# Cross-attention on one core: eighteen blocks of up to 128 query rows in place of twenty heads of 112, with q and k stacked through DRAM

## The reference

```python
q    = heads(x @ W_q)                      # 20 heads, 112 x 16
k_t, v_t = heads(text @ W_k), heads(text @ W_v)        # text: 371 rows
probs_t  = softmax(q @ k_t.T * 0.25)                   # 112 x 371 per head
text_out = probs_t @ v_t
k_ip, v_ip = heads(ip @ W_k_ip), heads(ip @ W_v_ip)    # ip: 4 rows
qsem = l2norm(probs_t @ text)                          # 112 x 512 per head
fused = q @ k_ip.T * 0.25 + 0.5 * qsem @ l2norm(ip).T  # 112 x 4 per head
ip_out = (softmax(fused) * mask) @ v_ip
out = (text_out + ip_out) @ W_out + b_out + x
```

## Time and profile before

| | us |
|---|---|
| median of 3 runs | 786.95 |
| the profiled execution | 787.76 |
| its span, first to last instruction | 786.0 |
| PE busy in the span | 752.7 (96%) |
| PE weight loads | 589.2 (75%) |
| DVE busy | 661.3 (84%) |
| ACT busy | 583.6 (74%) |
| POOL busy | 445.5 (57%) |
| mean granted TensorE clock | 0.984 of 2.4 GHz |
| DMA engines | queue of SyncE 44.66 MB, 21.9% of 16 engines |

### The profile page before, as it was taken

How to read it: one execution, slowest core, us unless ns; L and a number is a source line. 1 busy time by engine, 2 the same in 40 slices (tenths; PEclk the granted TensorE clock), 3 DMA queues, 4 the chain that set the end, 5 groups by cost and what they waited for, 6 DMA issues and landing times.

```text
span 786.0 us, 23801 instructions
## 1 busy us (share of the span) xinstructions
PE 752.7 (96%) x7730; PEld 589.2 (75%) x7730; DVE 661.3 (84%) x1960; ACT 583.6 (74%) x1702; POOL 445.5 (57%) x558
## 2 busy tenths in 40 slices
PE   5899999999999999999999999999999999999983
PEld 3568778787877878787787878778787777878661
DVE  4878898988989898898989889898998989889883
ACT  4378787877878787787878778787877878777770
POOL 4035574656647465664746566474656647464762
PEclk8999999999999999999999999999999999999996
DMA  8313222221412223140222314022231402021000
GB/s 268 100 50 74 73 68 61 61 79 43 104 27 67 63 58 81 42 107 24 68 65 57 83 41 107 21 70 65 54 87 38 109 22 69 19 52 42 9 2 15
DMA packets 71465, 50.02 MB, mean 64 GB/s; under 512 B 16640, under 2 KB 71280, under 8 KB 71344
## 3 DMA queue, kind: packets, MB, share of 16 engines
q1 hardware_dynamic: 67648, 44.66, 21.9%
q10 hardware_dynamic: 3696, 3.84, 1.7%
HBM read 20.80 MB, written 2.38 MB: 29 GB/s over the span
## 4 chain that ended last, share of the span: by engine, by line
PE 91%; issue 2%; DVE 2%; POOL 2%; DMA 1%; ACT 1%; ACTq 0%; SPq 0%; POOLq 0%; DVEq 0%
PE ps_prep L475 22%; PE ps_gram L574 19%; PE ps_pT L556 13%; PE ps_gram L575 12%; PE ps_score L548 6%; PE ps_prep L530 5%; PE ps_val L582 2%; PE ps_val L584 2%; PE ps_prep L527 1%; PE ps_prep L505 1%; PE ps_prep L610 1%; PE ps_prep L507 1%; DMA xt_sb<-in_x_t 1%; POOL dual L407 1%; POOL nrm L417 1%
## 5 line engine op out<-in xcount | busy, mean ns | idle before, releaser
L407 POOL TENSOR_TENSOR dual<-prob 112x371 f32<-112x371 f32 x320 | 282.9, 884 | 302.4 <-ACT prob L753 283.2
L574 PE MATMUL ps_gram<-gram_hi,pT_hi 125*128 125x371 f16 (+1 forms) x960 | 303.9, 320 | 0.0
L575 PE MATMUL ps_gram<-gram_lo,pT_hi 125*128 125x371 f16 (+2 forms) x960 | 255.9, 267 | 0.0
L747 ACT ACTIVATE pT_hi<-ps_pT 125x336 f16<-125x336 f32 x320 | 144.6, 452 | 143.4 <-PE ps_pT L556 139.9
L737 ACT ACTIVATE prob<-ps_score,low 112x371 f32<-112x371 f32 x320 | 184.0, 575 | 16.3 <-DVE low L912 9.8
L912 DVE TENSOR_REDUCE low<-ps_score 112x1 f32<-112x371 f32 x320 | 171.3, 535 | 28.5 <-PE ps_score L548 24.8
L917 DVE TENSOR_TENSOR pT_lo<-ps_pT,pT_hi 125x336 f16<-125x336 f32 x320 | 160.0, 500 | 38.2 <-ACT pT_hi L747 34.0
L927 DVE CUSTOM_DVE_ANT_0 quad_junk<-ps_gram,dual 112x371 f32<-112x371 f32 x320 | 171.1, 535 | 12.4 <-PE ps_gram L575 6.0
L753 ACT ACTIVATE prob<-prob 112x371 f16<-112x371 f32 x320 | 168.9, 528 | 0.0
L582 PE MATMUL ps_val<-val,pT_hi 125*128 125x42 f16 (+1 forms) x960 | 166.8, 182 | 0.0
L556 PE MATMUL ps_pT<-ident,prob 112*125 112x112 f32 x960 | 156.9, 272 | 5.6 <-DVE pT_lo L917 3.7
(11 more groups left out here) (183 smaller groups left out, 1405.8 us busy)
## 6 DMA issues: line engine op xcount, KB each, us to landing
ctx_sb<-in_ctx_t SPq DMA_DIRECT2D x15, 750.0 KB, 4.5
k_st<-k_lo SPq DMA_DIRECT2D x62, 70.3 KB, 2.1
k_st<-k_hi SPq DMA_DIRECT2D x60, 70.3 KB, 2.1
q_st<-q_hi SPq DMA_DIRECT2D x64, 48.0 KB, 2.0
k_st<-k_lo SPq DMA_DIRECT2D x62, 46.9 KB, 2.0
q_st<-q_lo SPq DMA_DIRECT2D x60, 48.0 KB, 2.0
k_st<-k_hi SPq DMA_DIRECT2D x60, 46.9 KB, 2.0
x_sb<-in_x SPq DMA_DIRECT2D x16, 140.0 KB, 2.4
```

Source lines behind the costliest of these rows:

```text
L407: nc.gpsimd.tensor_tensor(dual[:, h % 2, :], prob[:, h % 4, 0:TX], prob_16[:, h % 2, :], ALU.subtract).then_inc(s_dual, 1)
L574: nc.tensor.matmul(ps_gram[h % 2][:, 0:TX], hi, gh[0:TROWS[i], i, :], start=(i == 0), stop=False, skip_group_check=True)
L575: last = nc.tensor.matmul(ps_gram[h % 2][:, i * TC:TX], hi, gl[0:TROWS[i], i, i * TC:TX], start=False, stop=(i == NT - 1), skip_group_chec ...
```

## The change

A batch becomes 18 blocks. Blocks 0 to 17 are heads 0 to 17. Heads 18 and 19 are each cut in seven strips of 16 query rows, and blocks 0 to 13 carry one strip in rows 112 to 127, beside the 112 rows of their own head. A block of two heads takes its value products for both heads (84 and 42 columns, a strided slice of val), and its copy out of ps_val too. After block 13 the strips' values, quadratic forms and image scores are moved to their places by 14 DMAs (move_rows). q and k go to DRAM in four DMAs and come back in 24, 16 partitions at a time, into stacks where a strip's q and k stand in the 16 partitions beside the own head's; the masks and the second copies of q_hi and q_lo go. Values are copied out in four groups of 6, 6, 2 and 4 blocks. The order of the pieces, the steps of make, take, split, finish and soft are set anew for 18 steps: the last piece is a gram, made whole in step 16. The norms and powers of heads 0 to 13 are taken in steps 14 to 17 of their own batch, those of the other six in the next. k_st1 lies over w_raw. The start no longer stacks with DVE copies.

```diff
+NB = 18
+XR = P - S            # 16 rows
+XP = S // XR          # 7 strips
+NBX = HX * XP         # 14 blocks of two heads
+GROUPS = ((0, 6), (6, 12), (12, NBX), (NBX, NB))
-PIECE_Q, PIECES_K, PIECES_V, PIECES_G = 0, (1, 2, 3), (5, 7, 9), (4, 6, 8)
+PIECE_Q, PIECES_K, PIECES_V, PIECES_G = 0, (1, 2, 3), (5, 7, 8), (4, 6, 9)
+WHOLE = (PIECE_Q, PIECES_K[-1], PIECE_TURN_G)
-SPLIT_STEP = {2: 0, 4: 1, 6: 2, 8: 3, 10: 4}
+SPLIT_STEP = {2: 0, 4: 1, 7: 2, 9: 3, 11: 4}
-FINISH_STEP = {12: 0, 14: 1, 16: 2, 18: 3}
+FINISH_STEP = {11: 0, 13: 1, 15: 2, 17: 3}
+EARLY_VALS_STEP, EARLY_NORM_STEPS, EARLY_POWS = 14, (15, 15, 15, 16), {16: (0, EARLY // 2), 17: (EARLY // 2, EARLY)}
+VALS_STEP, POW_STEP, EXP_STEP = 0, 2, 6
+Q_OUT_STEP, Q_IN_STEP, K_OUT_STEP, K_IN_STEP, MOVE_STEP, LOAD_X_STEP = 2, 4, 7, 9, 14, 13
...
+        def stack_k(eng, a, term):
+            src, dst, p0 = k_bounce[a.odd, term % 2], k_st[a.odd], 32 * term
+            eng.dma_start(dst[p0:p0 + DH, :, :], src[0:NB * DH].rearrange("(t p) s -> p t s", p=DH)).then_inc(s_kst[a.odd], 16)
+            for e in range(HX):
+                eng.dma_start(dst[p0 + DH:p0 + 2 * DH, e * XP:(e + 1) * XP, :],
+                              src[(NB + e) * DH:(NB + e + 1) * DH].unsqueeze(1).to_broadcast([DH, XP, T])).then_inc(s_kst[a.odd], 16)
...
+            def bounce_k(a):
+                if a.n >= 2:
+                    sp.wait_ge(s_kst[a.odd], STACKED * a.pair)
+                sp.wait_ge(s_prep_hi, NM * a.n + place(a, PIECES_K[-1]) + 1)
+                sp.wait_ge(s_kip, a.n + 1)
+                k_to_dram(sp, a, 0)
                 sp.wait_ge(s_prep_lo, NM * a.n + place(a, PIECES_K[-1]) + 1)
+                k_to_dram(sp, a, 1)
+            def bring_k(a, term):
+                reached(sp, s_score, NB * (a.n - 1))
+                sp.wait_ge(s_stack, 1 + a.odd)
+                sp.wait_ge(s_k_out[term % 2], 16 * (a.n + 1))
+                stack_k(sp, a, term)
+            def move_rows(b):
+                sp.wait_ge(s_half, len(GROUPS) * b.n + 3)
+                sp.wait_ge(s_quad, NB * b.n + NBX)
+                sp.wait_ge(s_ip_score, NB * b.n + NBX)
+                reached(sp, s_vals, b.n)
+                for j in range(XP):
+                    q0 = j * XR
+                    sp.dma_start(raw[q0:q0 + XR, NB:H, 0:2 * VW], raw[S:P, j:NBX:XP, 2 * VW:BW]).then_inc(s_moved, 16)
+                    sp.dma_start(meta[b.odd][q0:q0 + XR, NB:H, :], meta[b.odd][S:P, j:NBX:XP, :]).then_inc(s_moved, 16)
...
             def end(f, step):
                 if step == VALS_STEP:
+                    pool.wait_ge(s_half, len(GROUPS) * (f.n + 1))
+                    pool.wait_ge(s_moved, MOVED * (f.n + 1))
+                    sum_values(EARLY, H).then_inc(s_vals, 1)
...
-                    last = nc.tensor.transpose(ps_pT[0:TC, i * S:(i + 1) * S], prob[:, h % 4, i * TC:(i + 1) * TC],
-                                               ident[0:S, 0:S])
+                    last = nc.tensor.transpose(ps_pT[0:TC, i * r:(i + 1) * r], prob[0:r, g % 4, i * TC:(i + 1) * TC], ident[0:r, 0:r])
...
+                heads = slice(t, NB + t // XP + 1, NB + t // XP - t) if t < NBX else slice(t, t + 1)
...
+                    nc.tensor.matmul(out_, pT_hi[0:r, t % 2, i, :], v[0:r, i, heads, :], start=(i == 0), stop=False, skip_group_check=True)
...
+                for t in range(NB):
+                    if prepare and t == Q_OUT_STEP:
+                        bounce_q(b.next())
+                    if prepare and 0 <= t - Q_IN_STEP < 2:
+                        for term in range(2):
+                            bring_q(b.next(), 2 * (t - Q_IN_STEP) + term)
...
             split_weight(w_hi[:, :, 1, :], w_raw[:, :, 1, :], s_w[1], 1)
-            act.wait_ge(s_prep_hi, place(start, PIECES_K[-1]) + 1)
-            act.wait_ge(s_kip, 1)
-            for dst, src in k_restack(0, (0, 2)):
-                act.dma_start(dst, src).then_inc(s_kst[0], 16)
+            act.wait_ge(s_stack, 1)
+            act.wait_ge(s_k_out[1], 16)
+            for term in (1, 3):
+                stack_k(act, start, term)
             make_hi(start, PIECES_V[0], SETUP_BANKS)
```

More of the change, by code:

```diff
@@ L65, with rows, group, column @@
 SOFT_NORMS, SOFT_ARGS = 4, 10
-TEXT_OUT_STEP = 8
+EARLY_STEPS = 1 + SOFT_NORMS
+TEXT_OUT_STEP = 4
 K_IP_STEP, RESIDUAL_STEP = 1, 11
-POW_HEADS = H // len(POW_STEPS)
-AHEAD_VALS_STEP, AHEAD_NORM_STEPS, AHEAD_POW_STEPS = 14, (15, 16, 17, 18), (18, 19)
+Q_OUT_STEP, Q_IN_STEP, K_OUT_STEP, K_IN_STEP, MOVE_STEP, LOAD_X_STEP = 2, 4, 7, 9, 14, 13
 S_PAD = P
 T_PAD = NT * P
+def rows(t):
+    return P if t < NBX else S
+def group(t):
+    return next(n for n, (t0, t1) in enumerate(GROUPS) if t0 <= t < t1)
+def column(t):
+    return (t - GROUPS[group(t)][0]) * BW
 def place(a, k):
@@ L157, in build @@
         val = [sb(f"val{i}", [TC, NT, H, 2 * VW], F16) for i in range(2)]
-        low = sb("low", [S, 4])
-        prob = sb("prob", [S, 4, T])
+        low = sb("low", [P, 4])
+        prob = sb("prob", [P, 4, T])
         pT_hi = sb("pT_hi", [TC, 2, NT, S_PAD], F16)
         pT_lo = sb("pT_lo", [TC, 2, NT, S_PAD], F16)
[L163 to L169, removed]
+        prob_16 = sb("prob_16", [P, 2, TX], F16)
+        dual = sb("dual", [P, 2, TX])
+        quad_junk = sb("quad_junk", [P, TX])
+        raw = sb("raw", [P, H, BW])
+        meta = [sb(f"meta{i}", [P, H, META]) for i in range(2)]
         vals = sb("vals", [S, H, VW])
@@ L415, in inverse_roots @@
-            def inverse_roots(part):
-                h0 = part * POW_HEADS
-                nc.gpsimd.tensor_tensor(nrm[:, 3, h0:h0 + POW_HEADS], nrm[:, 2, h0:h0 + POW_HEADS],
-                                        minus_half[0:S, 0:POW_HEADS], ALU.pow).then_inc(s_rn, 1)
-            def end(f, step, ahead=False):
-                if step == VALS_STEP:
[L422 to L425, removed]
-                    sum_values(f, 1).then_inc(s_vals, 1)
-                if step in POW_STEPS and not (ahead and POW_STEPS.index(step) * POW_HEADS < HH):
+                nc.gpsimd.tensor_tensor(dual[0:r, t % 2, :], prob[0:r, g % 4, 0:TX], prob_16[0:r, t % 2, :], ALU.subtract).then_inc(s_dual, 1)
@@ L1108, in body @@
-                    if not prepare and h in AHEAD_NORM_STEPS:
-                        norms_ahead(b, AHEAD_NORM_STEPS.index(h))
+                    if prepare and t in TAKE_STEP:
+                        make_lo(b.next(), TAKE_STEP[t])
+                    if finishing and t in FINISH_STEP:
+                        finish(b.last(), FINISH_STEP[t])
+                    softly(t, 1)
+                    quadratic(b, t)
+                    softly(t, 2)
+                    if turning and SPLIT_STEP.get(t) in DVE_PIECES:
+                        split_lo(b.next().next(), SPLIT_STEP[t])
```

458 lines of the change are left out of this document (233 added, 225 removed).

## The result

The changed kernel takes **804.42 us** (median of 4 runs, 800.89 to 807.7) where the kernel before takes 786.97 beside it: ratio 1.022, 95% interval 1.0175 to 1.0265. It is slower; the forecast was 760.2, faster, with 776 as the upper end. The profiled execution took 807.7 us on a span of 805.9; it is the longest of the four, 3.3 above the median. (PE is TensorE, SPq the queue of SyncE that issues transfers; landing is the end of a transfer as the profile has it.

What follows compares the result with a forecast made beforehand. PE (TensorE) was taken to bound the prepared batches. Start 42.14 + 5.5, fifteen batches 657.9, last batch 33.1 and tail 20.6 gave a span of 759.2, so a time of 760.2 us; range 747 to 776.

Steps and rivals of the forecast that it cites:

- PE's work per batch: Each of fifteen prepared batches: 46.02 - 2.84 for two steps gone + 0.28 transposes + 0.40 value products = 43.86 us.
- value pairs: Two-head value products on PE: 84 columns take 0.036 us, 42 stay at 0.025; 0.4 us a batch, bounds 0 and 2.1.
- Three wide transposes: PE's transposes with 128 moving columns instead of 112: 0.28 us a batch more, bounds nothing and 0.63.
- Rival 1: PE no longer saturated: chains through ps_pT and the late gram cost 0.3 to 1 us a batch; 770 us, chance 0.15.
- Rival 4: On PE, strided value operands double the pair, 2.1 us a batch instead of 0.4; 786 us, no change, chance 0.05.
- The step that failed: SyncE's queue, K stacks for the next batch: 12 issues end near 28 us, scores need K at 36; it fits.
- Rival 3: Stacks through DRAM come late, at the start and in batch 0: +7 us, 767, chance 0.09.
- The start: Before the first gram product: K lands near 39.5 us, +4.2, and lower clock 1.3; sum +5.5, bounds +3 and +9.
- Row moves: move_rows, 14 DMAs on SyncE's queue: land 11.9 us after step 14 began, in time with 0.9 us left.
- Rival 2: Moved rows arrive late for POOL and DVE if an issue costs over 0.71 us; at 0.9, 799 us, slower; chance 0.09.
- The last batch: Batch without preparation, now 35.16 us: 18 x 1.76 + 14 x 0.1 for wider buffers = 33.1 us.
- The tail: After the last quadratic: moves, sum, norms and one power of six heads end 2.2 us later, 20.6 us instead of 18.41.

Runs made afterwards that it cites:

- experiment 3: Changed kernel, bringing only columns 0 to 187 of the 375 of the stacked K from batch 2 on: 778.11 us, ratio 0.989 to the kernel before.
- experiment 5: Changed kernel with K brought in two portions, a semaphore each, the first score waiting only for the first: 762.19 us, ratio 0.9686 to the kernel before.
- experiment 6: Changed kernel with the rows of the q and k stacks two partitions apart instead of in a row: 767.98 us, ratio 0.975 to the kernel before.
- the first profile: The first profiled execution of the changed kernel, nothing further edited: 807.7 us on a span of 805.9.

## Why the prediction was wrong

**PE's work per batch: right.** 43.86 us was forecast, and 43.55 is what a batch takes without waits (experiments 3, 5 and 6). The value pairs grew as said: an 84-column product takes 0.038 us to the next start, for 0.036 forecast. Three wide transposes take 0.33 us to the next start in the batch of experiment 6, three narrow ones 0.32 in a batch before (means): +0.01 for +0.02 forecast. From the second to the third it is 0.109 us against 0.107, so the moving columns add next to nothing, near the lower of the two bounds. DVE at 39.5 (forecast 37.9), ACT at 34.2 (33.5) and POOL at 25.6 stayed beside PE, which is busy 43.57 of 43.57 us once K is in time. Rivals 1 and 4 fall.

**The step that failed** is in SyncE's queue: "its 12 issues end near 28, and scores need it at 36. Fits." The issues did end in time, even sooner (0.47 us apart, not 0.65). But the step counted issues and added no landing time that depends on bytes. It took for granted what small stacks showed, 2.0 us for one of 47 KB, where 12 transfers bring 1.54 MB, for which the last one needed 12.9 us. The earlier trace rows had another line to price bytes by: 750 KB of context land in 4.5 us. At that rate 1.54 MB are 9 us; counted from the first issue, near 20 by the forecast's own 28 less 12 issues, they would be in by 30, still ahead of 36. What no row of before held was the rate onto 16 partitions in a row: at 85 GB/s it is 18 us, in at 38, two too late. In the batch shown above K was wanted 34.8 us after the Q piece and there at 36.9. Rival 3 had the right place and the wrong size. It leaned on the write to DRAM (281 KB, which did land in 3.1 to 3.8 us) and gave +7; the return was the slow half. The 33.1 us of the fifteen batches are 25.9 of waits for K (7.4 of them in batch 1) and about 12 behind them, much of it at the lower clock, less 4.6 by which PE's own work was cheaper than foretold. For the batches the forecast had no price behind a wait. In batch 1 the stacks also left late: their first issue came 24.8 us after the Q piece, for 18.5 in batch 2, behind the 20 issues of v_ip, which the forecast had named with the start.

**The start: wrong by the same step.** "Landing near 39.5" was 49.88: 4.2 us foreseen, 14.5 measured. ACT's issues ended at 36.8, as forecast; the last landed 13 us later.

**Row moves: right.** Rival 2 would have begun to cost above 0.71 us an issue; it was 0.635, and nothing waited for the moves before the tail (experiment 6). The tail grew by 1.8 us for 2.2 forecast.

**The last batch: wrong by +2.4, of which 2.0 are a misplaced mark.** The forecast read 35.16 us for 20 heads, 1.76 each. From 730.46 on it is 37.12, or 1.86 each, and the forecast's own sum is then 18 x 1.86 + 1.4 = 34.8, for 35.46 measured. The same 2.0 us stood in the fifteen batches, which took 45.89 each and not 46.02 (43.73 instead of 43.86 forecast), so the whole sum hardly changes. The usual distance between two blocks grew from 1.72 or 1.73 to 1.83, the 0.1 of the forecast; the 0.6 left are in the longer ones among them, and their cause stays open.

**What is left with the rows apart.** The stretches of experiment 6 against the forecast are 6.7 us more at the start, 2.4 more in the last batch and 1.8 less in the others and the tail: 7.3 in all, its span of 766.5 against 759.2 (2.0 of the last two are the mark again). This only sorts the rest and is no test of the sum: the start still waits 12.0 us for K.

## What to carry to other kernels

When an edit turns many small transfers into a few large ones, price them by bytes over the rate of that destination, not by the landing time of a small one, and count the time from the first issue to the last landing. For transfers that write few partitions, look at which: rows two apart instead of in a row cut the way of K back from 17.5 to 12 us here, for the price of a slice and longer issues. And where a wait vanishes from a start, look for the next thing in the same queue before counting the gain.

## What the hardware showed that was not expected

- Writes to 16 partitions in a row ran at about half the rate of writes to 16 that lie 2, 4 or 8 apart (10.5 against 7.1 to 7.3 us for four transfers of 192,000 bytes; each further one landed 1.7 to 2.3 us after the one before, against 1.1 to 1.3), and 64 in a row were no faster than 32 (7.1 and 6.5).
- An issue of the same transfer took longer with the rows apart: 12 K issues in 8.9 us (382.54 to 391.43) in experiment 6, one of them a long one, and 7.1 to 8.4 us from the first start to the last for the batches 1 to 15, against 5.2 in most batches of the changed kernel. There SyncE's queue had room for it.
- The three long batches of the first profile had waits of 2.9, 2.1 and 2.7 us and lost 1.8 to 3.4 us more than these, with the granted clock at 0.50 in the one shown; batches with waits up to 1.5 us lost next to nothing more. How long the wait was does not decide it: without the moves one of 2.67 us cost only 0.2 more, with the granted clock at 1.00 behind it.
